# Where the first layer's eight result loads are issued: before or after the barrier between the two stages of a two-layer kernel on one core

## The reference, cut to what matters

```
x = x + mamba_block(layernorm(x))                      # first mixer
x = x + ffn(layernorm(x))                              # first layer's experts
x = x + attention_block(layernorm(x))                  # second mixer
x = x + ffn(layernorm(x))                              # second layer's experts

def ffn(x):
    topk_val, topk_idx = top_k(x @ gate_w + gate_b, 2)
    g = softmax(topk_val)
    y_e = gelu(x @ w1[e] + b1[e]) @ w2[e] + b2[e]      # for the two chosen experts e
    return g[0] * y_first + g[1] * y_second + x
```

## Time and profile before

| | |
|---|---|
| median of 3 runs | 762.06 us (758.38 to 765.02) |
| profiled execution, its own time | 761.67 us |
| its span in the trace | 759.7 us |
| around the span | 2.0 us |
| first stage | 0.7 to 355.8 us |
| second stage | 356.8 to 759.7 us |
| busy: PE, DVE, ACT, POOL | 82%, 66%, 54%, 54% of the span |
| TensorE's granted clock, mean | 0.906 of full speed |

### The profile page before, as it was taken

One profiled execution on the slowest core, in us unless ns is written; L12 is line 12 of the kernel. 1 busy time (PEld: TensorE's weight loads), 2 busy tenths in 40 slices (PEclk: granted clock), 3 DMA queues, 4 the chain that ended last, 5 costly groups with the idle time before them and its releaser, 6 DMA issues.

```text
span 759.7 us, 18411 instructions
## 1 busy us (share of the span) xinstructions
PE 625.5 (82%) x4637; PEld 440.6 (58%) x4637; DVE 502.2 (66%) x1488; ACT 411.6 (54%) x964; POOL 407.5 (54%) x482
## 2 busy tenths in 40 slices
PE   5878898997657999992886999999789449999990
PEld 2324344466426999992443455554456417999990
DVE  5769999775632665552698798997645614665544
ACT  2589999533202666661665576766653114566650
POOL 5328999956771555552685334443625762545550
PEclk9999999999766999996795799999999768999995
DMA  7637677496162222215356112110002172222216
GB/s 222 204 93 240 226 248 233 138 311 233 39 132 51 79 71 71 72 47 145 87 200 219 45 46 67 44 54 14 2 1 105 47 130 65 75 71 73 72 37 173
DMA packets 81993, 85.08 MB, mean 112 GB/s; under 512 B 14248, under 2 KB 59432, under 8 KB 81656
## 3 DMA queue, kind: packets, MB, share of 16 engines
q1 hardware_dynamic: 72824, 70.94, 31.1%
q0 software_dynamic: 5632, 11.58, 4.9%
q10 hardware_dynamic: 3456, 1.59, 1.1%
HBM read 61.53 MB, written 22.54 MB: 111 GB/s over the span
## 4 chain that ended last, share of the span: by engine, by line
PE 34%; DVE 6%; issue 3%; DMA 3%; POOL 3%; ACT 2%; SPq 2%; DVEq 0%; POOLq 0%; ACTq 0%
PE bank L661 7%; PE bank L670 7%; PE bank L2204 5%; PE bank L2135 3%; DVE t_peak L1955 3%; PE bank L2138 2%; PE bank L2314 2%; PE bank L2180 2%; POOL xrows L418 2%; PE bank L2305 2%; PE bank L654 1%; DVE X L255 1%; DMA xrows<-t_front,t_e_slot 1%; DMA work<-results 1%; SPq L1614 1%
## 5 line engine op out<-in xcount | busy, mean ns | idle before, releaser
L1955 DVE TENSOR_REDUCE t_peak<-bank 128x1 f32<-128x512 f32 (+2 forms) x192 | 104.0, 591 | 10.1 <-PE bank L2138 7.8
L462 ACT ACTIVATE m_dx_tiles<-bank,m_e_b1all 128x128 f32<-128x128 f32 x224 | 64.1, 368 | 53.5 <-PE bank L661 53.4
L462 ACT ACTIVATE t_v_tiles<-bank,t_e_b1all 128x128 f32<-128x128 f32 x224 | 64.1, 369 | 51.4 <-PE bank L661 41.2
L426 POOL DMA_INDIRECT results<-m_XC,m_e_to_row x56 | 53.9, 962 | 66.7 <-DVE m_XC L577 64.2
L426 POOL DMA_INDIRECT results<-t_A,t_e_to_row x56 | 53.8, 961 | 65.9 <-DVE t_A L577 62.2
L864 POOL TENSOR_TENSOR UN<-m_tabs,w1all 128x512 f32<-128x512 f32 x64 | 84.8, 1357 | 5.6 <-DVE m_tabs L1194 4.7
L1365 PE MATMUL bank<-UN,ident 128*128 128x512 f32 x128 | 69.1, 629 | 9.2 <-POOL UN L864 7.8
L567 DVE COPY UN<-w1all 128x512 f32 x112 | 48.0, 429 | 42.3 <-PE bank L661 35.4
L661 PE MATMUL bank<-m_XC,UN 128*128 128x128 f32 x448 | 60.9, 280 | 0.0
L670 PE MATMUL bank<-w2all,m_dx_tiles 128*128 x448 | 60.2, 278 | 0.6 <-DVE m_XC L577 0.6
L661 PE MATMUL bank<-t_A,UN 128*128 128x128 f32 x448 | 60.5, 279 | 0.0
(11 more groups left out here) (326 smaller groups left out, 1414.0 us busy)
## 6 DMA issues: line engine op xcount, KB each, us to landing
w1all<-bc_rows SPq DMA_DIRECT2D x64, 256.0 KB, 4.1
w2all<-bc_rows SPq DMA_DIRECT2D x26, 256.0 KB, 4.1
w1all<-in_e_w SPq DMA_DIRECT2D x6, 1024.0 KB, 11.6
work<-results SPq DMA_DIRECT2D x16, 256.0 KB, 4.9
m_dx_tiles<-xrows SPq DMA_DIRECT2D x56, 64.5 KB, 1.8
t_v_tiles<-xrows SPq DMA_DIRECT2D x56, 64.5 KB, 1.8
t_tabs<-stacks SPq DMA_DIRECT2D x32, 96.0 KB, 2.1
work<-stacks SPq DMA_DIRECT2D x32, 96.0 KB, 2.2
```

What stands on the lines that cost most here:

```text
L426: g.indirect_dma_start(core.results, bass.IndirectOffsetOnAxis(e.to_row[:, j:j + 1], 0), e.ysb[:, j % 4, :], None).then_inc(core.y_out[j % ...
L462: ins = act.activation(e.hid[:, mp, f * P:f * P + P], core.tiles(2 + mp)[:, f, :], ACT.Gelu, bias=row(e.b1all, x)[:, f:f + 1])
L1955: v.tensor_reduce(peak[p][:, a, ss[0]:ss[-1] + 1, qt], bank[:, f, 0:len(ss) * w].rearrange("p (j n) -> p j n", n=w), AX_X, ALU.max).then_i ...
```

## The change

The wait for `y_out` and the eight loads go into a function of their own, `load_back`. The second layer calls it where the code stood before. For the first layer it is no longer called at the end of the first stage's SP stream but at the start of the second stage's, ahead of the 25 loads. The counts that are waited for are the same.

```diff
+def load_back(core, sp, layer):
+    for q in range(4):
+        sp.wait_ge(core.y_out[q], 16 * SLOT_TILES // 4 * layer)
+    results = core.results.rearrange("(t p) d -> p t d", p=P)
+    for b in range(NB):
+        for k in range(TOPK):
+            sp.dma_start(core.back[k][:, b * TT:b * TT + TT, :],
+                         results[:, k * NT + b * TT:k * NT + b * TT + TT, :]).then_inc(core.back_in[b], 16)
@@ Experts.sync
         e.steps(sp, step)
-        for q in range(4):
-            sp.wait_ge(core.y_out[q], e.counted + 16 * SLOT_TILES // 4)
-        results = core.results.rearrange("(t p) d -> p t d", p=P)
-        for b in range(NB):
-            for k in range(TOPK):
-                sp.dma_start(core.back[k][:, b * TT:b * TT + TT, :],
-                             results[:, k * NT + b * TT:k * NT + b * TT + TT, :]).then_inc(core.back_in[b], 16)
         if e.layer == 2:
+            load_back(core, sp, 2)
             for b in range(NB):
@@ attention, @block.sync
         def _(sp):
+            load_back(core, sp, 1)
             for dst, name in ((vec, "vec_b"), (wqkv, "wqkv")):
                 sp.dma_start(dst[:], io[name]).then_inc(qkv_in, 16)
```

## The result

| | before | after |
|---|---|---|
| median | 764.16 us (20 runs) | 767.25 us (20 runs) |
| ratio, 95% interval | | 1.0043 (1.0029 to 1.0057) |
| profiled execution, its span | 761.67, 759.7 | 767.73, 765.8 |

The change costs 0.43%, some 3.3 us. The interval leaves out 1, so the loss is real, and it stays inside the 1% that the prediction took as what few runs can tell from no change. The median of before stands here over 20 runs and not 3, and is 2.1 us above the one that the prediction started from.

The account below looks back on a forecast made before the run. POOL's drain was taken to set the barrier, and DVE's first `combine` the second stage; 0 + 0.15 + 3.92 - 0.04 = +4.03 us on 761.67 gave 765.7, as a median 766.1, range 761.0 to 770.0.

Parts of the forecast that it names:

- POOL's drain sets the barrier, and the loads lie in its shadow: First stage's end: POOL arrives last, by 0.5 us, so removing SP's eight loads there gains 0.
- Four waits, 0.15: SP behind the barrier: four already satisfied waits cost only their issue, 0.15 us, bounded by 0.1 to 0.4.
- The pair's landing, 3.92: Second stage's start: batch 0's two result loads, now exposed, delay `combine` by 3.92 us, bounded by 3.5 and 4.5.
- Sum +4.03: Whole kernel: 0 + 0.15 + 3.92 - 0.04 = +4.03 us, 765.7 for the profiled execution, 766.1 for the median.
- Batches 1 to 3 of `combine`: DVE in the second stage: last load lands at 367.0, batch 3 is due at 371.6; nothing added.
- The weights' slack: 25 loads behind the eight: begin 5.5 us later, users 4.03 later; 1.5 slack lost, cost 0, up to 1 us.
- The third rival: Eight result loads and projection's three share DMA engines; ACT waits 1 to 2 us, whole 767 to 768; chance 0.09.
- The clock: TensorE in the second stage: rise to full speed comes 4 us later, near 375.5; cost 0, bounded by -2.5 and +2.5.
- The second rival: TensorE's clock rises two or more batches later in the work; 771.1 at two, slower by over 1%; chance 0.04.

Follow-up runs that it names:

- early-drain run: Kernel before plus a second POOL drain between the 32 scatters of the rows and the 56 of the results; ratio 1.0007 (0.9981 to 1.0033).
- no drains, before: Kernel before with neither the first stage's block nor the small block draining POOL, both barriers kept; ratio 1.0010 (0.9983 to 1.0038).

## Why the prediction was right, point by point

- **POOL's drain sets the barrier, and the loads lie in its shadow: right.** 8.440 without loads, SP 26 us early, release unmoved. The evidence it went by, two drains that differ by one nanosecond with different loads beside them, held. SP's drain was foreseen near 335 to 347 and came at 329.0: the reason given was right, SP gets there when its last slot load is issued, but in the kernel before that load begins at 326.3, and no row stood behind the times. And "wholly in its shadow" is true of the execution that was read, by 0.5 us; by the 6.11 us of the early-drain run it need not be true of every one.
- **Four waits, 0.15: right,** 0.12 (SP's first load comes 9.56 us behind the last scatter, where the first weight load came 9.44 behind it).
- **The pair's landing, 3.92: right,** 3.85, and the pair's second load landed after the same 3.4 us. The Trainium skill's formula (2.0 us and bytes over 436 GB/s, "DMA: Bandwidth & Descriptors", section on the anatomy of one DMA) is fitted on the GpSimd path. As an estimate for these loads of SP it stayed too low here as well: 2.6 against the 2.9 of the first load and the 3.4 of the second.
- **Sum +4.03: right,** +3.93 in the profile; 3.3 by the ratio, whose interval, 2.2 to 4.4 us, holds it. The time came out at 767.25, 1.1 above the forecast, by two misses that partly cancel: the median of before rose by 2.1 with more runs, and the medians lie 3.1 apart and not 4.0.
- **Batches 1 to 3 of `combine`: right,** no wait, 3.52 to 3.55 apart.
- **The weights' slack: the size was off.** The eight issues took 6.17 us, not 5.5 (the last alone up to 1.9). The projection's third load was issued at 366.80 and landed 4.4 later, at 371.2, 8.1 us after `combine` and not 6.6 to 8.0. ACT started at 371.52 and the transposes that it also needs ended at 371.43, so the slack was used up to 0.2 us and nothing was paid, though the profile puts ACT's wait down to this load and not, as foreseen, to the same as before. The third rival was that near. SP's own wait on q and k shrank from 14.6 to 10.9, more than the 1.5 foreseen, with much to spare.
- **The clock: bounded well, its course foreseen wrong.** Windows of the kernel after (columns as in rows 9):

```profile
366.00:369.00 3.00, 3.00 (x4) 0.68 (x3) 2.90 (x14) 0.00 (x0) 1.89 (x4) 0.50 1.11 273
369.00:370.00 1.00, 0.29 (x1) 0.00 (x0) 0.96 (x5) 0.93 (x3) 0.03 (x1) 0.88 0.40 105
...
372.00:373.00 1.00, 0.65 (x1) 0.30 (x2) 0.97 (x5) 0.71 (x3) 0.47 (x2) 0.82 1.03 347
373.00:374.00 1.00, 1.00 (x3) 0.38 (x2) 0.97 (x9) 1.00 (x4) 0.10 (x1) 0.50 0.48 111
...
376.00:377.00 1.00, 1.00 (x11) 1.00 (x10) 0.93 (x6) 0.65 (x2) 0.34 (x2) 0.97 0.87 178
```

  The granted clock rose to full speed already near 369.2, at the end of the 3.8 us of unread matmuls, fell to half near 372.6 after PE had been busy for 0.9 of 3 us, and rose again near 376.0. Counted from `combine`, that later rise is at 12.9 us, where the only one was at 14.6. The early stretch sped up the first transposes (0.66 us in place of 1.11) and took 0.26 us off the first projection (1.82 in place of 2.08), and POOL's rotation began 13.59 us after `combine` and not 14.31. The whole remainder doesn't show these 0.7 us (402.7 against 402.8), but it scatters by more. The second rival didn't come.

## What to carry to other kernels

Before moving work away from in front of a barrier, look who arrives there last: a hole in which only one queue is seen issuing is not proof that this queue holds the barrier. Loads behind the last writes belong in front of a barrier that is late anyway, and only those that the next stage reads first; the rest cost a few tenths of a microsecond behind it here. And moving the loads has the other sign once the cover is gone, so it is to be tried again when the barrier has been made faster: here by leaving out POOL's drains, in a kernel where SP waits for all results before the barrier.

## What the runs showed of the hardware

A drain of POOL behind 88 indirect DMAs (32 and 56) cost 7.25 us of its own in the first layer, with POOL idle and the transfers landed (7.247, 7.252), and 0.04 when another drain stood just before. In the second layer it took 8.44, as in the first with the last scatter still to run. With a drain in between, the one behind 56 cost 4.6, in proportion. The proportion is not a law: the early one, behind 32, took 5.7 instead of 2.6; and where both drains of the first stage were left out, the second stage's, with all 176 indirect DMAs since the last drain, took 8.69 instead of 8.44, where the proportion would give 14.5 and more. This is that drain in the run "no drains, before":

```profile
L1590 POOLq DRAIN  x1: 8692/8692/8692, 742.6 to 742.6; - x1
```

What the drain does in this time, what bounds it behind 176, and why the early one was so long stay open.
